# An attention phase whose row maxima run fourteen steps ahead of the scores instead of sixteen, with the layout of each tile's maxima moved inside the preceding tile

## The reference

```python
attn = jax.nn.softmax(jnp.einsum('bhqd,bhkd->bhqk', q, k) * scale, axis=-1)   # 16384 queries, 320 keys, 4 heads
out = jnp.einsum('bhqk,bhkd->bhqd', attn, v)
out = out.transpose(0, 2, 1, 3).reshape(b, n, c)
out = out @ proj_w + proj_b
```

## Time and profile before

| | |
|---|---|
| three executions | 11576.59, 11580.47, 11598.01 us |
| profiled execution, own time | 11584.36 us |
| its span | 11582.8 us |
| mean granted TensorE clock | 0.978 |
| busy: TensorE, VectorE, ScalarE, GpSimd | 90%, 76%, 63%, 24% of the span |
| row-maximum reductions, L978 | 4096 of 818 ns |
| maxima matmuls, L714 | 8192 of 302 ns |
| scores, L735 | 4096 of 386 ns |

### The profile page before, as it was taken

How to read it: one execution, slowest core, us unless ns; L and a number is a source line. 1 busy time by engine, 2 the same in 40 slices (tenths; PEclk the granted TensorE clock), 3 DMA queues, 4 the chain that set the end, 5 groups by cost and what they waited for, 6 DMA issues and landing times. The chain is left out here.

```text
span 11582.8 us, 198561 instructions
## 1 busy us (share of the span) xinstructions
PE 10455.8 (90%) x71885; PEld 5275.3 (46%) x72029; DVE 8796.4 (76%) x15082; ACT 7250.1 (63%) x12109; POOL 2763.8 (24%) x5217
## 2 busy tenths in 40 slices
PE   2898998989989899899989989899898998989999
PEld 1544445344454544535445354444534445354453
DVE  7877777777777777778777787777777777777776
ACT  5667565675656757567575666756567565675756
POOL 2313213122131221312223131221312213122130
PEclk9999999999999999999999999999999999999999
DMA  2021221212213022130211302122121221202213
GB/s 65 20 47 46 47 64 29 49 35 51 60 31 59 31 48 56 35 61 34 42 51 42 69 20 47 46 47 64 30 52 32 52 59 32 57 31 50 54 37 74
DMA packets 176857, 537.70 MB, mean 46 GB/s; under 512 B 64904, under 2 KB 87560, under 8 KB 154448
## 3 DMA queue, kind: packets, MB, share of 16 engines
q1 hardware_dynamic: 175952, 525.31, 20.1%
HBM read 232.49 MB, written 71.30 MB: 26 GB/s over the span
## 5 line engine op out<-in xcount | busy, mean ns | idle before, releaser
L978 DVE TENSOR_REDUCE R<-ps 128x2 f32<-128x640 f32 x4096 | 3185.4, 818 | 906.3 <-PE ps L714 904.8
L1185 ACT ACTIVATE R<-ps 128x512 f32<-128x512 f32 x5120 | 2821.4, 594 | 654.5 <-PE ps L735 628.9
L258 ACT ACTIVATE R<-R,st 128x1475 bf16<-128x1475 f32 (+1 forms) x1326 | 2077.1, 1566 | 489.6 <-DVE st L330 464.9
L319 DVE TENSOR_SCALAR_CACHE_REDUCE R<-R,st 128x1255 bf16<-128x1255 f32 (+1 forms) x1326 | 1936.8, 1461 | 18.5
L714 PE MATMUL ps<-KST,R 96*128 96x320 bf16 x8192 | 1811.8, 302 | 38.8 <-DVE R L978 29.5
L760 PE MATMUL ps<-R 128*32 128x512 f32 x12288 | 1641.0, 607 | 37.9 <-DVE Wk L931 32.8
L735 PE MATMUL ps<-R,KST 104*128 104x512 bf16 x4096 | 1569.6, 386 | 36.9 <-ACT R L1185 23.7
L714 PEld LDWEIGHTS ps<-KST,R 96*128 96x128 bf16 x8192 | 757.6, 99 | 736.6 <-DVE R L978 223.8
L1268 POOL CAST R<-Wk 128x512 bf16<-128x512 f32 x256 | 283.8, 1109 | 2492.7 <-DVE Wk L931 2492.7
L735 PEld LDWEIGHTS ps<-R,KST 104*128 104x128 bf16 x4096 | 395.7, 97 | 724.3 <-ACT R L1185 461.3
L384 POOL TENSOR_TENSOR R<-R,sB 128x1024 f32<-128x1024 f32 x132 | 251.3, 1924 | 1641.4 <-DMA R<-xh_in 1635.9
(11 more groups left out here) (211 smaller groups left out, 19167.0 us busy)
## 6 DMA issues: line engine op xcount, KB each, us to landing
R<-R SPq DMA_DIRECT2D x3072, 64.0 KB, 2.4
R<-xh_in SPq DMA_DIRECT2D x136, 512.0 KB, 4.4
out_dram<-Z SPq DMA_DIRECT2D x68, 1024.0 KB, 3.9
R<-xa_in SPq DMA_DIRECT2D x36, 1024.0 KB, 10.0
R<-xb_in SPq DMA_DIRECT2D x36, 1024.0 KB, 12.0
R<-sr_in SPq DMA_DIRECT2D x32, 1024.0 KB, 5.1
R<-sr_in SPq DMA_DIRECT2D x16, 2016.0 KB, 9.2
R<-sr_in SPq DMA_DIRECT2D x16, 1056.0 KB
```

The lines of the kernel that those rows point to most:

```text
L258: e.activation(junka[:, 0:o2 - o1], xc[:, o1:o2], ACT.Sign, bias=mid, scale=-1.0, accum_out=ca[i]).then_inc(md_ca, 1)
L319: e.tensor_scalar(junk[:, 0:o1 - o0], xc[:, o0:o1], mid, None, ALU.is_le, ALU.add, accum_out=cv[i]).then_inc(md_cv, 1)
L978: e.tensor_reduce(MX[(4 * u + s4) % 2][:, blk_, h0:h0 + 2], ps[:, 2 + 2 * bq:4 + 2 * bq, 0:320], axis=AX.X, op=ALU.max).then_inc(mx, 1)
L1185: e.activation(PB[:, t % 2, w, :], ps[:, w % 2, :], ACT.Exp).then_inc(ex, 1)
```

## The change

The maxima's steps run 14 ahead of the scores, not 16: in w = 0 and 1 of tile t stand the last two steps of tile t + 1, in w = 2 to 7 the first six of tile t + 2. `split_max` of tile t + 1 follows step w = 1 of tile t on VectorE. `lay_max` of tile t + 1 stands at w = 3 of tile t on TensorE and ScalarE, and in SyncE's queue at the head of tile t as before, now from tile 0 on. Ahead of the first tile stand 14 steps, with the layout of tile 0 after the tenth. The last two steps of an image are in tile 30.

```diff
--- before.py
+++ after.py
@@ -18,7 +18,7 @@
 KH = 65
 STEPS = 26
 WAITS = 4
-AHEAD = 2
+LEAD = 14
 WEIGHS = (2, 4, 7)
 STAGES = {(0, 2): (1, 0, 6), (0, 6): (1, 1, 6), (1, 4): (1, 2, 6), (1, 9): (1, 3, 7),
           **{(8 * g - 12 + j, 9): (g, j, 7) for g in (2, 3) for j in range(4)}}
@@ -787,23 +787,24 @@
                 op.then_inc(po_ps, 1)
                 b6[0] = (zo, t + 1)
 
-            for t in range(AHEAD):
-                for i in range(8):
-                    maxima(0, t, i)
-                    busy(0, 2)
-                lay_max(t)
+            for g in range(LEAD):
+                maxima(0, g // 8, g % 8)
+                busy(0, 2)
+                if g == 9:
+                    lay_max(0)
             for t in range(NT + 2):
-                u, s4, ahead = t // 4, t % 4, t + AHEAD
+                u, s4 = t // 4, t % 4
                 live, prev, done2 = t < NT, 0 <= t - 1 < NT, t >= 2
                 for w in range(10):
                     if live:
                         scores(t, w)
                     if t == 0 and w == 8:
                         values()
-                    if w < 8 and live and ahead < NT:
-                        maxima(ahead // 4, ahead % 4, w)
-                    if w == 1 and t and t + AHEAD - 1 < NT:
-                        lay_max(t + AHEAD - 1)
+                    g = 8 * t + LEAD + w
+                    if w < 8 and g < 8 * NT:
+                        maxima(g // 32, g // 8 % 4, g % 8)
+                    if w == 3 and t + 1 < NT:
+                        lay_max(t + 1)
                     if w in WEIGHS and prev:
                         weigh(t - 1, WEIGHS.index(w))
                     if w in (4, 6) and t == NT + 1:
@@ -1023,22 +1024,23 @@
                     e.wait_ge(zb, 4)
                 e.tensor_tensor(zo_, ps[:, 6, 0:256].rearrange("p (w c) -> p c w", w=4), zo_, ALU.add).then_inc(zo, 1)
 
-            for t in range(AHEAD):
-                for i in range(8):
-                    maxima(0, t, i)
-                split_max(t)
+            for g in range(LEAD):
+                maxima(0, g // 8, g % 8)
+                if g == 7:
+                    split_max(0)
             for t in range(NT + 2):
-                u, s4, ahead = t // 4, t % 4, t + AHEAD
+                u, s4 = t // 4, t % 4
                 live, prev, done2 = t < NT, 0 <= t - 1 < NT, t >= 2
                 for w in range(10):
                     if w == 0 and done2:
                         denominators(t - 2)
                     if w == 7 and done2:
                         project_out(t - 2)
-                    if w < 8 and live and ahead < NT:
-                        maxima(ahead // 4, ahead % 4, w)
-                    if w == 8 and live and ahead < NT:
-                        split_max(ahead)
+                    g = 8 * t + LEAD + w
+                    if w < 8 and g < 8 * NT:
+                        maxima(g // 32, g // 8 % 4, g % 8)
+                        if g % 8 == 7:
+                            split_max(g // 8)
                     if t == NT - 1 and w in (1, 4):
                         e.wait_ge(in_xc[0], 32)
                         largest(e, w // 4)
@@ -1336,12 +1337,11 @@
                 e.dma_start(QS[u % 3][96:104, :, 512 * s4:512 * s4 + 512],
                             MR[t % 2].unsqueeze(1).to_broadcast([8, 4, 512])).then_inc(in_m[t % 2], 16)
 
-            for t in range(AHEAD):
-                lay_max(t)
+            lay_max(0)
             for t in range(NT):
                 u, s4 = t // 4, t % 4
-                if t and t + AHEAD - 1 < NT:
-                    lay_max(t + AHEAD - 1)
+                if t + 1 < NT:
+                    lay_max(t + 1)
                 if u == 6:
                     if s4 == 0:
                         e.wait_ge(q_ps, 16)
```

## The result

The changed kernel takes 11927.77 us (median of five executions, 11912.65 to 11942.95) against 11580.47: a ratio of 1.0295, 95% interval [1.0281, 1.0309]. The direction of the forecast and its mechanism inside the tiles hold. Its time, 11844, is 84 us too low, and the measurement lies 33 us above the range: most of what is missing lies between the images, where the forecast had no term.

What follows compares the result with a forecast made beforehand. TensorE's order was taken as the bound, except from the turn to the maxima of w = 2, where VectorE sets the time. Per image 9 x 1.18 + 15 x 0.41 - 0.6 + 0 + 0.3 = 16.5 us, 264 in 16: 11844, range 11,795 to 11,895.

Steps and rivals of the forecast that it cites:

- a start of 0: Ahead of the first tile and in tile 0, gains and losses were taken to sum to 0 us.
- the stage tiles' 24: Upper end for the nine stage tiles an image: 1.35 us each instead of the forecast 1.18.
- the four tiles' 32: Upper end for tiles 25 to 28: always held like a stage tile, +1.4 us an image instead of -0.6.
- the start's 40 us: Upper end for the start of the images, forecast at 0 with ends of -40 and +40 us.
- The layout moves out of its cover: In 15 ordinary tiles an image, transposes at w = 3 no longer lie under VectorE's chain: +0.41 us each.
- Nine tiles with GpSimd: In tiles 2, 5 to 8 and 13 to 16, GpSimd's subtraction holds the split's cast: +1.18 us each.
- GpSimd doesn't hold the split: Rival for the nine stage tiles, 20%: the hold is absent, 111 us less, 11,733 us.
- Four tiles lose a hold: In tiles 25 to 28 GpSimd's median additions mostly stop holding the split: 2.6 against 3.3 lost, -0.6 us an image.
- Tile 30: The tile with two steps more and its layout later: +0.3 us an image.
- Start of an image: Ahead of the first tile and in tile 0: 0 us in sum, with ends of -40 and +40.
- The score starts no earlier: In 11 of 16 images the first score still waits for the first maxima's DMA, despite two steps saved.
- The clock that I weighed at +26 at most: A longer wait before the first score may cost a slow-clock stretch, up to 16 x 1.6 = +26 us.

Runs made afterwards that it cites:

- e1: The kernel before with only the layout of the maxima moved, to w = 3 instead of w = 1: 11751.73 us, ratio 1.0143.
- e11: The kernel before with the layout of the maxima at w = 2 instead of w = 1: 11697.29 us, ratio 1.0103.
- e2: The changed kernel with GpSimd's subtraction of a stage at w = 9 waiting for the split: 11812.13 us, ratio to the kernel before 1.0186.
- e4: The kernel before with GpSimd's median additions in the attention waiting for the split at w = 8: 11500.61 us, ratio 0.9928.
- e3: The changed kernel with twenty filler matmuls behind the fourteen steps ahead of the first tile: 11833.16 us, ratio to the kernel before 1.0213.
- e5: The changed kernel with four fillers more, between its fourteen steps and tile 0: 11857.03 us, ratio to the kernel before 1.0243.
- e6: The kernel before without the four fillers behind the first two of its sixteen steps: 11635.72 us, ratio 1.0048.
- e9: The changed kernel with four fillers more in the DFT part (16 for 12 at L557): 11885.01 us, ratio to the kernel before 1.0266.

## Why the prediction was wrong, and where it was right

The forecast had +264 us, the two traces differ by 344. The step that failed is the sum: it had no term for the jump between images, which took 61.8, and a start of 0, which took 29. The tiles took 242.6, 21 less than told, and 10.5 lie elsewhere. The jump alone would carry 11844 above 11,895. The range was also narrower than the ends that it names: the stage tiles' 24, the four tiles' 32 and the start's 40 us, added to 11844, reach 11,940.

- **The layout moves out of its cover: right.** +0.41 an ordinary tile forecast, +0.43 measured (+0.42 in e1), with the maxima of w = 2 at 2.27 us behind the turn; e1 shows it alone. That 0.41 is the price beside a score; beside a weighing it is 0.18 (e11).
- **Nine tiles with GpSimd: right.** +1.18 forecast, +1.09 measured, of which e2 takes 0.67 away. The rival "GpSimd doesn't hold the split" is out, although the two start 0.01 us apart. The Trainium skill (SBUF — State Buffer, "SBUF: two separate sides") speaks of a lock for the whole instruction; the cast of 1.18 us, ending 0.04 behind GpSimd's, agrees.
- **Four tiles lose a hold: right in direction, too small.** -0.6 forecast (its own terms, 2.6 - 3.3, give -0.7), 41.3 - 42.8 = -1.5 measured, as means of 16 images. The hold had cost 42.8 - 39.2 (e4) = 3.7 and not 3.3, and what is left of it is 0.5 and not 0.95: the cast takes 0.4 to 0.9 us in three of the tiles and at most 0.3 in the fourth.
- **Tile 30:** +0.3 forecast, +0.27 measured.
- **Start of an image: mis-sized, "I take 0, with ends of -40 and +40".** It is -4.0 + 33.2 = +29 us. "The score starts no earlier" nearly held: it comes 0.25 us earlier, and waits 4.8 us for its DMA in all 16 images. Tile 0 is then 45.5 us longer and tile 1, which stands in none of my lists, 12.2 shorter. The clock that I weighed at +26 at most was the larger part: (1 - granted clock) x length, summed over tile 0, is 32 us before and 71 in the changed kernel, and e3, which fills the wait, gains 51 us behind the first score and pays 12 ahead of it. I had the rows for the direction and chose the middle. The Trainium skill (TensorE: Matmul & The Clock Gate, part 1) has the clock halved by default and freed by activity. I gave that its own sentence and no weight; the scores of 0.61 us behind the wait agree.
- **The jump between images: the step that was missing.** The sum went over tiles and the start and had no term for the loop itself: +61.8 us by the trace, and 59 either way in e5 and e6. I had counted the fillers that go as time saved in a wait, not as instructions. The Trainium skill (Runtime: NRT & Kernel Launch, "Instruction fetch mechanics") says that code streams in blocks of 16 KiB, 256 instructions, fetched one ahead, and that a taken branch to a block outside the two-block window waits for its fetch. The packets of 16.4 KB and their place at the jump agree; where the blocks' bounds lie in this code no run here shows. I hadn't brought that page to a change that removes eight TensorE instructions an image.
- The remaining 10 us lie in code that no part of the change touches. The same stretches are 12 us shorter than before in e4 and 20 longer in e5, so I give them no cause.

What stays open: why e4 gains 20 us at the start, and what sets the packet's place to the instruction. That TensorE waits for this packet rests on its timing in 75 jumps, not on a run that moves the packet alone. The cost of the missing fillers doesn't depend on it: e5, e6 and e9 show that by themselves.

## What to carry to other kernels

An operation beside a chain of another engine is free only as far as that chain reaches; measure from the chain's start to its last waiter (2.27 us here) and keep the operation inside. A change that drops or adds instructions in a loop moves the code against the jump back: compare the gap at the loop's end before crediting or blaming the new order. Where TensorE comes early to a long wait, fillers in that wait can keep its clock up (e3). And when two engines share a lock, let the long one wait for the short one, as in e4, the fastest kernel here.

## What the runs showed of the hardware that was not expected

- The restart of TensorE at the loop's end took 1.5 to 1.8 us in most turns (up to 2.5 in some), or 2.4 to 4.3 us in all, by four fillers among some 110 in an image; with the slower clock behind it that is 4 us a turn of the loop.
- Four transposes of 128 x 8 cost TensorE 0.18 us between maxima and a weighing (e11) and 0.40 between maxima and a score (e1).
- A cast of 16 elements a partition was held for as long as GpSimd's 128 x 512 subtraction though it began 0.01 us behind it: 1.18 us for 0.18.
